# Splitting the last two groups' second-layer products into high and low parts

## The chip, the cores and the metric

The kernel runs on one core of a Trainium2 chip. The metric is the device time of one execution in microseconds (us). Before the change the median of three runs is 255.69 us (255.53 to 255.90).

## What is computed

A vision tower with one block: patches of 32 images are projected to 192 channels and a class token is put in front (37 rows an image); a bidirectional recurrence (RWKV's wkv) and a squared-ReLU layer follow as "attention"; then a mixture of 16 experts, 4 chosen for each row, with a shared expert. The change concerns the second matrix of each expert, which turns 96 hidden values back into 192 channels:

```python
c = (jax.nn.one_hot(idx, E, dtype=w.dtype) * w[..., None]).sum(1)      # routing weights
h = jax.nn.silu(jnp.einsum('th,ehi->tei', x, gWg) + gbg) * (jnp.einsum('th,ehi->tei', x, gWu) + gbu)
out_e = jnp.einsum('tei,eih->teh', h, gWd) + gbd                       # second layer
moe_out = jnp.einsum('te,teh->th', c, out_e)
hs = jax.nn.silu(x @ sWg + sbg) * (x @ sWu + sbu)
shared = hs @ sWd + sbd                                                # second layer, shared
return (moe_out + shared).reshape(orig_shape)
```

All of it is float32.

## The kernel before, in words

The rows are worked on in four groups of 6, 10, 10 and 6 images: groups 0 and 3 have 222 rows in 2 row tiles of 112, groups 1 and 2 have 370 rows in 3 row tiles of 124. Each group passes through stages, and each engine interleaves the stages of several groups:

- **F** (front): patches, first norm, the projections k, v, r (PE), the recurrence with its scans (DVE) and exponentials (ACT), and the output projection.
- **M** (mid): second norm, the squared-ReLU layer (`up`, `mix`), third norm, router logits and the choice of experts (many short DVE operations, the last is `routed`).
- **G** (PE): the first layer of the experts in 14 units of 128 hidden values, unit 0 and 1 the shared expert's (`sgu`), 2 to 13 the experts' (`egu`). `g n` is unit n's gate product, `v n` its value product. Each is five passes over a stack of high and low parts (`from_stack`): operands of type float32r, one pass each in the trace; a float32 product shows as two.
- **Y** (ACT): `e n`, SiLU of the gate. **S** (DVE): `s n`, value times gate into `hid`, which has two slots, n % 2. **X** (DVE): `x n`, times the routing weights that a DMA has spread over the partitions (`gates`); `end` adds the result to the residual `h1`.
- **D** (PE): `d n`, the second layer of unit n, the sum over the units in the PSUM banks `PA`. Its operands are plain float32, 192 weight columns stream against each row tile of `hid`. `cT` transposes the routing weights, which then go to DRAM and come back as `gates`.

The order on each engine is written out by hand in the lists `PE_ORDER`, `ACT_ORDER` and `DVE_ORDER`: "S3:s5" is step s5 of group 3. Each engine works its list off strictly, semaphores are waited for where a step needs data. Unit `v n+1` on PE can only start when `s n` has emptied its PSUM bank, `g n+1` when `e n` has.

`H` steps are products of constants into an unused bank, between PE's first steps (`pe_heat`).

Of the kernel before, what the change touches and what calls it, by code (L numbers as in the profile page):

```python
# [5 lines left out]
F32, F32R = mybir.dt.float32, mybir.dt.float32r  # L6
# [73 lines left out]
BY_PE = 2  # L80


def build(nc, A):
    ctx = ExitStack()
    with ctx:
# [80 lines left out]
        K, V, R = (sb(n, [128, WK]) for n in ("K", "V", "R"))  # L166
        mx = sb("mx", [128, 2 * (WK + 2) + 2 * WK])
        E1 = sb("E1", [128, 2 * (WK + T)])
        S = sb("S", [128, 4 * WS + 2])
        top = sb("top", [128, WK])  # L170
# [35 lines left out]
        c_pad = sb("c_pad", [TP, TILES, CPAD])  # L206

# [76 lines left out]
        out_ready = counted("out_ready", 1)  # L284
        out_stored = [sem(f"out_stored{g}") for g in range(len(GROUP))]
# [300 lines left out]

        def act_gates(act_e, g):
# [216 lines left out]
        def dve_mid(v, g):  # L804
# [13 lines left out]
            if g >= 2:  # L818
                v.wait_ge(out_stored[g - 2], 16 * GROUP[g - 2].tiles)
# [110 lines left out]
        def dve_weighed(v, g):  # L930
# [7 lines left out]

            v.wait_ge(pe_down, at(pe_down, g, UNITS))
            for bank, a, b in G.banks:  # L940
                h = h1[g % 2][0:G.tp, a:b, :]
                last = V_.tensor_tensor(h, h, rows(PA, G, bank, a, b), ALU.add)
            last.then_inc(out_ready, 1)
            yield "end"

        @block.vector
        def _(v):
# [19 lines left out]
            advance(tracks_of(v, dve_low_parts, F=dve_front, M=dve_mid, S=dve_gated, X=dve_weighed), DVE_ORDER)  # L967
# [78 lines left out]
        def pe_heat(pe):  # L1046
# [25 lines left out]
            yield "rstd"  # L1072
            pe.wait_ge(front_step[0], 5)
# [168 lines left out]
        def pe_downs(pe, g):  # L1242
# [6 lines left out]
            if g:  # L1249
                pe.wait_ge(out_ready, at(out_ready, g, 0))  # L1250
            else:
                split(pe, len(PIECES))
            for n in DOWNS:
                if n < SCH:
# [12 lines left out]
                down(G, PA, src, w, n == DOWNS[0], n == DOWNS[-1]).then_inc(pe_down, 1)  # L1267
# [11 lines left out]
def _order(*parts):  # L1279
# [146 lines left out]
```

## Time and profile before

| | |
|---|---|
| median of 3 runs | 255.69 us |
| the profiled execution | 255.63 us |
| its span in the trace | 253.5 us |
| PE busy | 242.6 us, 96% |
| DVE busy | 191.4 us, 76% |
| ACT busy | 151.0 us, 60% |
| POOL busy | 17.9 us, 7% |
| chain that ended last | PE 73%, ACT 9%, DVE 8%, issue 4% |

The table is read so: PE has work nearly all the time, and it makes up most of the chain of waits. Busy time of PE is modelled from the start of each pass, so that short waits between passes don't show in it; starts of neighbouring passes show them. DVE's share is an average over a first half in which it is nearly full and a second half in which it is not. 2.1 us of the execution's time lie outside the span.

### The profile page before, as it was taken

What the parts mean: (1) busy time and instruction counts of PE and PEld (TensorE: products, weight loads), DVE (VectorE), ACT (ScalarE), POOL (GpSimd) and SP (SyncE); (2) the same over time, 40 slices, a digit from 0 to 9 for tenths busy, and PEclk for the clock granted to TensorE, in tenths of its full rate; (3) what the DMA queues carried; (4) which work ended last, traced back from release to release, by engine and by line L of the source; (5) the groups of instructions that cost most, each with busy time, mean ns of one, the idle gap of its engine ahead of it and who ended that gap; (6) DMA issues with size and microseconds to landing.
All of it is one profiled execution on the core that took longest, in us unless ns stands there. A gap on an engine that the chain in (4) does not pass through costs nothing.

```text
span 253.5 us, 4370 instructions
## 1 busy us (share of the span) xinstructions
PE 242.6 (96%) x1508; PEld 222.6 (88%) x1508; DVE 191.4 (76%) x490; ACT 151.0 (60%) x311; POOL 17.9 (7%) x29
## 2 busy tenths in 40 slices
PE   8789899899999999999999999999999999999994
PEld 7677477677588899999999999999999999999993
DVE  5489988999989999999797799877323275843442
ACT  2797899978769999735767862335631341232220
POOL 6100302003101000101100001010000010000000
PEclk9997999999999999999999999999999999999999
DMA  6958271100000430000005510000354000014510
GB/s 170 332 176 309 85 243 62 38 0 0 0 3 10 106 94 13 0 3 0 1 11 157 185 43 1 1 3 0 82 173 136 18 3 0 1 40 92 102 33 27
DMA packets 13165, 17.46 MB, mean 69 GB/s; under 512 B 2359, under 2 KB 11224, under 8 KB 13016
## 3 DMA queue, kind: packets, MB, share of 16 engines
q1 hardware_dynamic: 12872, 17.08, 22.7%
q8 instruction: 12, 0.20, 0.3%
q10 hardware_dynamic: 272, 0.11, 0.2%
q14 instruction: 9, 0.07, 0.1%
HBM read 16.20 MB, written 0.99 MB: 68 GB/s over the span
## 4 chain that ended last, share of the span: by engine, by line
PE 73%; ACT 9%; DVE 8%; issue 4%; DMA 3%; SPq 2%; POOL 0%; DVEq 0%; POOLq 0%
PE PA L998 16%; PE PG L978 16%; PE PG L980 11%; PE PF L998 7%; PE PQ L978 4%; PE PQ L980 3%; PE PX L1029 2%; DMA gates<-c_rows 2%; PE PQ L1049 2%; PE PF L988 1%; PE PG L1149 1%; PE PG L1148 1%; DMA gates<-in_w_k 1%; ACT norm L422 1%; PE PF L1013 1%
## 5 line engine op out<-in xcount | busy, mean ns | idle before, releaser
L584 ACT ACTIVATE act<-PG,columns 128x222 f32<-128x222 f32 (+3 forms) x56 | 28.4, 507 | 58.8 <-PE PG L980 55.1
L978 PE MATMUL PG<-stack,hi_egu 128*128 128x222 f32 (+1 forms) x288 | 62.2, 324 | 0.0
L927 DVE SCALAR_TENSOR_TENSOR hid<-PG,columns,act 128x222 f32<-128x222 f32 (+1 forms) x52 | 27.3, 524 | 28.3 <-PE PG L980 24.8
L998 PE MATMUL PA<-w_ed,hid 128*124 128x192 f32 (+1 forms) x240 | 46.3, 328 | 0.4 <-DVE hid L936 0.3
L978 PEld LDWEIGHTS PG<-stack,hi_egu 128*128 128x128 f32 x288 | 45.6, 190 | 0.7 <-DVE hid L927 0.2
L980 PE MATMUL PG<-stack,lo_egu 128*128 128x222 f32 (+1 forms) x192 | 42.7, 304 | 0.0
L998 PEld LDWEIGHTS PA<-w_ed,hid 128*124 128x124 f32 (+1 forms) x240 | 38.5, 183 | 1.2 <-DVE hid L936 1.2
L980 PEld LDWEIGHTS PG<-stack,lo_egu 128*128 128x128 f32 x192 | 31.8, 190 | 0.0
L396 POOL TENSOR_TENSOR rstd<-var,minus_half 112x2 f32<-112x2 f32 (+3 forms) x12 | 13.9, 1156 | 186.8 <-DVE var L671 186.8
L936 DVE TENSOR_TENSOR hid<-hid,gates 128x222 f32<-128x222 f32 (+1 forms) x48 | 21.9, 462 | 1.8 <-DMA gates<-c_rows 0.9
L998 PE MATMUL PF<-w_down,mix_hid 128*124 128x192 f32 (+1 forms) x120 | 22.8, 326 | 0.0
L998 PEld LDWEIGHTS PF<-w_down,mix_hid 128*124 128x124 f32 (+1 forms) x120 | 19.5, 182 | 0.3 <-issue 0.2
L754 DVE TENSOR_TENSOR_SCAN S<-E,S 128x333 f32<-128x333 f32 (+1 forms) x16 | 16.2, 1064 | 0.3 <-ACT E L501 0.2
L978 PE MATMUL PQ<-stack,hi_up 128*128 128x222 f32 (+1 forms) x72 | 15.3, 321 | 0.0
L1049 PE MATMUL PQ<-still 128*128 128x256 f32 x36 | 11.8, 488 | 2.5 <-ACT h L450 1.4
L552 ACT ACTIVATE relu<-PQ 128x222 f32<-128x222 f32 (+1 forms) x24 | 9.9, 415 | 5.4 <-PE PQ L980 5.3
L1042 PE MATMUL PA<-gates,columns 128*128 128x512 f32 x24 | 12.4, 598 | 0.7 <-ACT lo_egu L414 0.7
L1049 PEld LDWEIGHTS PQ<-still 128*128 128x128 f32 x36 | 8.8, 256 | 4.5 <-ACT h L450 1.8
L778 DVE RECIPROCAL K<-K 128x222 f32<-128x222 f32 (+3 forms) x8 | 12.2, 1531 | 0.1
L978 PEld LDWEIGHTS PQ<-stack,hi_up 128*128 128x128 f32 x72 | 11.3, 191 | 0.3
L422 ACT ACTIVATE norm<-h,shift,rstd 124x192 f32<-124x192 f32 (+1 forms) x20 | 9.6, 538 | 3.1 <-DVE shift L678 3.0
L558 ACT ACTIVATE mix_hid<-relu 128x222 f32<-128x222 f32 (+1 forms) x24 | 10.8, 451 | 0.8
(248 smaller groups left out, 443.1 us busy)
## 6 DMA issues: line engine op xcount, KB each, us to landing
gates<-in_w_egu SPq DMA_DIRECT2D x6, 512.0 KB, 4.8
gates<-c_rows SPq DMA_DIRECT2D x16, 138.8 KB, 2.9
gates<-c_rows SPq DMA_DIRECT2D x16, 92.5 KB, 2.8
gates<-c_rows SPq DMA_DIRECT2D x16, 83.2 KB, 2.4
w_ed<-in_w_ed SPq DMA_DIRECT2D x1, 1152.0 KB, 8.0
gates<-c_rows SPq DMA_DIRECT2D x16, 55.5 KB, 2.6
gates<-in_w_up SPq DMA_DIRECT2D x2, 384.0 KB, 4.0
pat<-in_patches SPq DMA_DIRECT2D x2, 370.0 KB, 4.1
```

The lines of the kernel that those rows point to most:

```text
L396: nc.gpsimd.tensor_tensor(small[n]["rstd"][0:G.tp, 0:cols, 0:G.tiles], small[n]["var"][0:G.tp, 0:cols, 0:G.tiles], minus_half[0:G.tp, 0:co ...
L422: last = nc.scalar.activation(norm[n][0:G.tp, t, :], x[0:G.tp, t, :], ACT.Identity, bias=small[n]["shift"][0:G.tp, col, t:t + 1], scale=sm ...
L584: nc.scalar.activation(act[128 - gate:128, n % 2, 0:G.n], PG[0:gate, gate_bank(n), 0:G.n], ACT.Silu, bias=bias).then_inc(act_silu, 1)
L754: step(V_.tensor_tensor_scan(run(x, d), run(E1[:, d * WK:d * WK + wk], d), run(x, d), 0.0, ALU.mult, ALU.add))
L778: step(V_.reciprocal(K[:, s], K[:, s]))
L927: V_.scalar_tensor_tensor(out, PG[part, 1, 0:G.n], bias, act[part, i, 0:G.n], ALU.add, ALU.mult).then_inc(mul_done, 1)
L936: V_.tensor_tensor(out, out, gates[:, n - SCH, 0:G.n], ALU.mult).then_inc(hid_ready, 1)
L978: mm(out, w_hi[:, slot, cols], x[:, p, 0:G.n], start=(p == 0), stop=False, skip_group_check=True)
L980: last = mm(out, w_lo[:, p, cols], x[:, p, 0:G.n], start=False, stop=(p == 1), skip_group_check=True)
L998: last = mm(tile_out(P, G, t), src[:, G.ts[t]:G.ts[t] + G.tp], w, start=start and t != 1, stop=stop, skip_group_check=True)
L1042: mm(PA[:, s, 0:cols], ident32, raw[n % RING][:, s * cols:(s + 1) * cols], start=True, stop=False)
L1049: mm(PQ[:, 0:256], still[:, 0:128], still[:, :], start=True, stop=True, skip_group_check=True)
```

## The change

1. For groups 2 and 3 (`SPLIT`), the second layer of units 1 to 13 (group 2) and 1 to 12 (group 3) is computed from float32r parts. ACT copies `hid` to `hid_hi` (rounded), DVE subtracts it from `hid` into `hid_lo`. The weights are split once in the same way into `w_both`, whose 384 columns are the high part and the low part side by side. A row tile then takes two passes: `hid_hi` against all 384 columns, `hid_lo` against the 192 columns of the high part. High-times-high and low-times-high add up in the first 192 columns, high-times-low in the next 192. Unit 0 of both groups and unit 13 of group 3 stay in float32.
2. The two halves are added to the residual apart: a new step `low` and the old `end`. Unit 13 of group 3, which writes the bank that `low` reads, waits for `low`. The third row tile of group 2 now has the bank `PX` to itself.
3. `hid` slots come free when `hid_lo` has been made, no longer when the product is done.
4. The buffers of the recurrence share their memory with `w_both`, `hid_hi` and `hid_lo`, so the weights are split after the last group's recurrence.
5. `gated` of groups 2 and 3 no longer waits for the stores of two groups before; `h1` behind it does.
6. Five more `H` steps stand among PE's first steps, and one of them no longer waits.
7. The three lists are written anew from the first mid stage on.

```diff
+SPLIT = (2, 3)
+SPLIT_UNITS = {2: [1, *range(2, UNITS)], 3: [1, *range(2, UNITS - 1)]}
+BLOCKS = ((1, 2), (2, 6), (6, 10), (10, 14))
...
+        w_both = sb("w_both", [128, UNITS - 1, 2 * C], F32R)
+        hid_hi, hid_lo = (sb(n, [128, 2, N], F32R) for n in ("hid_hi", "hid_lo"))
...
+        def wide_out(G, t, cols):
+            return (PA[0:G.tp, t, cols] if t < 2 else PX[0:G.tp, cols])
...
+        def act_split(act_e, g):
+            if g == SPLIT[0]:
+                act_e.wait_ge(z_ready, at(z_ready, LAST, 1))
+                for i, (a, b) in enumerate(BLOCKS):
+                    nc.scalar.activation(w_both[:, a - 1:b - 1, 0:C], whole_downs(a, b), ACT.Copy).then_inc(w_high, 1)
+                    yield f"w{i}"
+            for n in SPLIT_UNITS[g]:
...
+                nc.scalar.activation(hid_hi[:, n % 2, 0:G.n], hid[:, n % 2, 0:G.n], ACT.Copy).then_inc(hid_high, 1)
+                yield f"h{n}"
...
+        def dve_split(v, g):
+            if g == SPLIT[0]:
+                for i, (a, b) in enumerate(BLOCKS):
+                    v.wait_ge(w_high, i + 1)
+                    V_.tensor_tensor(w_both[:, a - 1:b - 1, C:2 * C], whole_downs(a, b), w_both[:, a - 1:b - 1, 0:C].bitcast(F32), ALU.subtract).then_inc(w_both_in, 1)
+                    yield f"w{i}"
+            for n in SPLIT_UNITS[g]:
+                v.wait_ge(hid_high, split_count(g, n))
...
+                V_.tensor_tensor(hid_lo[:, n % 2, 0:G.n], hid[:, n % 2, 0:G.n], hid_hi[:, n % 2, 0:G.n].bitcast(F32), ALU.subtract).then_inc(hid_low, 1)
+                yield f"l{n}"
+            v.wait_ge(pe_down, down_count(g, SPLIT_UNITS[g][-1]))
+            for h, bank in wide_sums(G, g):
+                last = V_.tensor_tensor(h, h, bank[:, :, C:2 * C], ALU.add)
+            last.then_inc(low_added, 1)
+            yield "low"
...
             for n in DOWNS:
+                if g in SPLIT and n in SPLIT_UNITS[g]:
+                    pe.wait_ge(hid_low, split_count(g, n))
+                    for t in range(G.tiles):
+                        here = slice(G.ts[t], G.ts[t] + G.tp)
+                        mm(wide_out(G, t, slice(0, 2 * C)), hid_hi[:, n % 2, here], w_both[:, n - 1, :], start=n == DOWNS[0], stop=False, skip_group_check=True)
+                        last = mm(wide_out(G, t, slice(0, C)), hid_lo[:, n % 2, here], w_both[:, n - 1, 0:C], start=False, stop=n == DOWNS[-1], skip_group_check=True)
+                    last.then_inc(pe_down, 1)
+                    yield f"d{n}"
+                    continue
...
+                if g in SPLIT:
+                    if n and n not in SPLIT_UNITS[g]:
+                        pe.wait_ge(low_added, g - SPLIT[0] + 1)
...
-    "G3:g9 D3:d7 G3:v9 G3:g10 D3:d8 G3:v10 G3:g11 D3:d9 G3:v11 G3:g12 D3:d10 G3:v12 G3:g13 D3:d11 G3:v13 D3:d12 D3:d13",
+    "G3:g8 D3:d5 G3:v8 G3:g9 D3:d6 G3:v9 G3:g10 D3:d7 G3:v10 G3:g11 D3:d8 G3:v11 G3:g12 D3:d9 G3:v12 D3:d10 G3:g13 G3:v13",
+    "D3:d11 D3:d12 D3:d13",
```

What the lists do to the instructions at two places. First PE's last instructions, before: the two G rows in front are `v13` of group 3, the last row `d12` and `d13` together (two row tiles each).

```order
L998 MATMUL PA<-w_ed,hid 112x192 x2
L978 MATMUL PG<-stack_1,hi_egu 128x222 x3
L980 MATMUL PG<-stack_1,lo_egu 128x222 x2
L998 MATMUL PA<-w_ed,hid 112x192 x4
L85 UNCONDITIONAL_BRANCH
```

And now, from `v13` on:

```order
L1063 MATMUL PG<-stack_1,hi_egu 128x222 x3
L1065 MATMUL PG<-stack_1,lo_egu 128x222 x2
L1349 MATMUL PA<-w_both,hid_hi 112x384
L1350 MATMUL PA<-w_both,hid_lo 112x192
L1349 MATMUL PA<-w_both,hid_hi 112x384
L1350 MATMUL PA<-w_both,hid_lo 112x192
L1349 MATMUL PA<-w_both,hid_hi 112x384
L1350 MATMUL PA<-w_both,hid_lo 112x192
L1349 MATMUL PA<-w_both,hid_hi 112x384
L1350 MATMUL PA<-w_both,hid_lo 112x192
L1371 MATMUL PA<-w_ed,hid 112x192 x2
```

`d11` has moved from before `v13` to behind it, so that two split units stand between `v13` and the float32 unit `d13`.

DVE's last instructions, before (`s12`, `x12`, `s13`, `x13`, `end`):

```order
L927 SCALAR_TENSOR_TENSOR hid<-PG,columns,act 128x222
L936 TENSOR_TENSOR hid<-hid,gates 128x222
L927 SCALAR_TENSOR_TENSOR hid<-PG,columns,act 128x222
L936 TENSOR_TENSOR hid<-hid,gates 128x222
L942 TENSOR_TENSOR h_1<-h_1,PA 112x384
```

And now (`s11`, `x11`, `s12`, `x12`, `l11` and `l12`, `s13`, `x13`, `low`, `end`):

```order
L981 SCALAR_TENSOR_TENSOR hid<-PG,columns,act 128x222
L990 TENSOR_TENSOR hid<-hid,gates 128x222
L981 SCALAR_TENSOR_TENSOR hid<-PG,columns,act 128x222
L990 TENSOR_TENSOR hid<-hid,gates 128x222
L1023 TENSOR_TENSOR hid_lo<-hid,hid_hi 128x222 x2
L981 SCALAR_TENSOR_TENSOR hid<-PG,columns,act 128x222
L990 TENSOR_TENSOR hid<-hid,gates 128x222
L1027 TENSOR_TENSOR h_1<-h_1,PA 112x384
L1004 TENSOR_TENSOR h_1<-h_1,PA 112x384
```

The subtractions of two units stand together behind both of their `x` steps, and `low` comes between `x13` and `end`.

The last place is DVE between groups 1 and 2, before (`s13`, `x13`, `end` of group 1, then `s0` to `s3` and `x2` of group 2):

```order
L927 SCALAR_TENSOR_TENSOR hid<-PG,columns,act 128x370
L936 TENSOR_TENSOR hid<-hid,gates 128x370
L942 TENSOR_TENSOR h_1<-h_1,PA 124x384
L942 TENSOR_TENSOR h_1<-h_1,PA 124x192
L927 SCALAR_TENSOR_TENSOR hid_s<-PG,columns,act 64x370
L927 SCALAR_TENSOR_TENSOR hid<-PG,columns,act 128x370 x2
L936 TENSOR_TENSOR hid<-hid,gates 128x370
```

And now:

```order
L981 SCALAR_TENSOR_TENSOR hid<-PG,columns,act 128x370
L990 TENSOR_TENSOR hid<-hid,gates 128x370
L981 SCALAR_TENSOR_TENSOR hid_s<-PG,columns,act 64x370
L997 TENSOR_TENSOR h_1<-h_1,PA 124x384
L997 TENSOR_TENSOR h_1<-h_1,PA 124x192
L981 SCALAR_TENSOR_TENSOR hid<-PG,columns,act 128x370
L1015 TENSOR_TENSOR w_both<-w_ed,w_both 128x4x192 x2
L1023 TENSOR_TENSOR hid_lo<-hid,hid_hi 128x370
L981 SCALAR_TENSOR_TENSOR hid<-PG,columns,act 128x370
```

Two of the four weight subtractions and `l1` now stand between `s1` and `s2` of group 2; the other two stand further ahead, in the choice of experts of group 2.

## Rows read from the trace of the kernel before

**Rows 1.** Stretch: length, busy us of PE, PEld, DVE, ACT, POOL, clock, DMA
```profile
50.00:75.00 25.00, 23.97 (x134) 18.03 (x134) 23.60 (x54) 19.53 (x40) 3.01 (x2) 1.00 0.01 1
75.00:100.00 25.00, 24.28 (x166) 23.09 (x165) 24.22 (x55) 23.80 (x46) 0.85 (x1) 1.00 0.25 57
...
150.00:175.00 25.00, 25.00 (x158) 24.89 (x157) 21.71 (x76) 10.33 (x21) 1.54 (x2) 1.00 0.00 1
...
200.00:225.00 25.00, 25.00 (x158) 24.65 (x156) 16.07 (x56) 6.67 (x15) 0.93 (x1) 1.00 0.01 2
225.00:253.50 28.50, 24.71 (x188) 23.56 (x186) 12.27 (x29) 5.79 (x13) 0.00 (x0) 1.00 0.30 65
```

**Rows 2.** The same view at the start of the kernel, same columns
```profile
20.00:22.00 2.00, 2.00 (x7) 1.55 (x6) 1.97 (x10) 1.68 (x4) 0.00 (x0) 0.52 0.54 217
```

**Rows 3.** Chain of waits, float32 second-layer units: start us, us, engine and line
```profile
203.37 0.97 PE PA L998 x6
...
233.03 0.65 PE PA L998 x4
```

**Rows 4.** Groups by form, PE's weight loads: count, then busy us and mean ns
```profile
L998 PEld LDWEIGHTS PA<-w_ed,hid 128*124 128x124 f32 x144 | 23.7, 187 | 0.2 <-DVE hid L936 0.2
```

**Rows 5.** Timeline of PE, float32r passes, group 2: start us, us
```profile
132.31 0.47 PE L988 MATMUL PF<-hi_rf,stack 128*124 128x192 f32 x3
...
132.84 0.49 PE L988 MATMUL PF<-hi_rf,stack 128*124 128x192 f32 x3
...
134.80 0.68 PE L978 MATMUL PG<-stack,hi_egu 128*128 128x370 f32 x3
...
135.66 0.68 PE L978 MATMUL PG<-stack,hi_egu 128*128 128x370 f32 x3
```

**Rows 6.** The same view, float32r passes with 112 weight columns, group 3
```profile
177.66 0.46 PE L988 MATMUL PF<-hi_rf,stack 128*112 128x192 f32 x3
...
178.15 0.51 PE L978 MATMUL PQ<-stack,hi_up 128*128 128x222 f32 x3
```

**Rows 7.** Groups by form, DVE and ACT: count, busy us, mean ns
```profile
L936 DVE TENSOR_TENSOR hid<-hid,gates 128x370 f32<-128x370 f32 x24 | 12.9, 541 | 0.5
...
L619 DVE TENSOR_TENSOR lo_up<-gates,hi_up 128x768 fp32r<-128x768 f32 x2 | 1.8, 954 | 0.2 <-ACT hi_up L405 0.2
```

**Rows 8.** The same view of ACT
```profile
L558 ACT ACTIVATE mix_hid<-relu 128x370 f32<-128x370 f32 x12 | 6.2, 513 | 0.4
...
L584 ACT ACT_TABLE_LOAD x4 | 5.1, 1283 | 0.1
...
L558 ACT ACTIVATE mix_hid<-relu 128x222 f32<-128x222 f32 x12 | 4.7, 390 | 0.4
```

**Rows 9.** Timeline of one period in group 3 (v, s, next v)
```profile
238.66 0.62 PE L978 MATMUL PG<-stack,hi_egu 128*128 128x222 f32 x3
...
239.54 0.45 DVE L927 SCALAR_TENSOR_TENSOR hid<-PG,columns,act 128x222 f32<-128x222 f32 x1 [0.89 <-PE PG L980]
...
240.42 0.62 PE L978 MATMUL PG<-stack,hi_egu 128*128 128x222 f32 x3
```

**Rows 10.** Timeline where group 3's units begin (g1's last passes, v1)
```profile
225.35 0.38 PE L980 MATMUL PG<-stack,lo_sgu 128*128 128x222 f32 x2
...
225.81 0.59 PE L978 MATMUL PG<-stack,hi_sgu 128*128 128x222 f32 x3
```

**Rows 11.** Timeline of the end (d12, s13, x13, d13, end)
```profile
248.14 0.81 PE L998 MATMUL PA<-w_ed,hid 128*112 128x192 f32 x4
248.34 0.45 DVE L927 SCALAR_TENSOR_TENSOR hid<-PG,columns,act 128x222 f32<-128x222 f32 x1 [0.88 <-PE PG L980]
248.83 0.39 DVE L936 TENSOR_TENSOR hid<-hid,gates 128x222 f32<-128x222 f32 x1
249.27 0.90 PE L998 MATMUL PA<-w_ed,hid 128*112 128x192 f32 x4 [0.32 <-DVE hid L936]
250.21 0.55 DVE L942 TENSOR_TENSOR h<-h,PA 112x384 f32<-112x384 f32 x1 [1.00 <-PE PA L998]
```

More of the change, by code:

```diff
@@ L164, in build @@
             ("rstd", [TP, 2, TILES]), ("shift", [TP, 2, TILES]))) for i in "123")]
[L166 to L170, printed above, removed]
         Zm = sb("Zm", [128, N])
@@ L206, in build, with early @@
         c_pad = sb("c_pad", [TP, TILES, CPAD])
+        with ExitStack() as recurrence_space:
+            def early(name, shape):
+                return recurrence_space.enter_context(nc.sbuf_tensor(name, shape, F32))
+            K, V, R = (early(n, [128, WK]) for n in ("K", "V", "R"))
+            mx = early("mx", [128, 2 * (WK + 2) + 2 * WK])
+            E1 = early("E1", [128, 2 * (WK + T)])
+            S = early("S", [128, 4 * WS + 2])
+            top = early("top", [128, WK])
+        w_both = sb("w_both", [128, UNITS - 1, 2 * C], F32R)
+        hid_hi, hid_lo = (sb(n, [128, 2, N], F32R) for n in ("hid_hi", "hid_lo"))
         PF = pb("PF", [128, 2, 512])
@@ L292, in tile_out, with whole_downs, wide_sums, split_count @@
             return P[0:G.tp, t // 2, (t % 2) * C:(t % 2 + 1) * C]
+        def whole_downs(a, b):
+            return whole["sd"][:, a:b, :] if a < SCH else whole["ed"][:, a - SCH:b - SCH, :]
+        def wide_out(G, t, cols):
+            return (PA[0:G.tp, t, cols] if t < 2 else PX[0:G.tp, cols])
+        def wide_sums(G, g):
+            pairs = (h1[g % 2][0:G.tp, 0:2, :], PA[0:G.tp, 0:2, :]), (h1[g % 2][0:G.tp, 2:3, :], PX[0:G.tp, None, :])
+            return pairs[:G.tiles - 1]
+        def split_count(g, n):
+            return sum(len(SPLIT_UNITS[k]) for k in SPLIT if k < g) + SPLIT_UNITS[g].index(n) + 1
+        def down_count(g, n):
+            return at(pe_down, g, DOWNS.index(n) + 1)
         def advance(tracks, order):
@@ L824, in dve_mid @@
             settle()
+            if g >= 2:
+                v.wait_ge(out_stored[g - 2], 16 * GROUP[g - 2].tiles)
             step(V_.scalar_tensor_tensor(h[rs], gate_r[rs], 0.5, base[g % 2][rs], ALU.mult, ALU.add))
@@ L922, in dve_gated @@
                     since(v, hid_ready, g)
+                elif g in SPLIT:
+                    v.wait_ge(hid_low, split_count(g, n - 2))
                 else:
@@ L1054, in pe_heat @@
                 yield f"early{n}"
-            pe.wait_ge(tok_out, 1)
-            spin()
-            yield "tok"
+            for n in range(4):
+                spin()
+                yield f"tok{n}"
             pe.wait_ge(front_step[0], 1)
@@ L1072, in pe_heat @@
             yield "rstd"
+            for after in ("kt", "rt"):
+                spin()
+                yield after
             pe.wait_ge(front_step[0], 5)
@@ L1266, in pe_downs @@
                     src, w = hid[:, n % 2, :], whole["ed"][:, n - SCH, :]
-                down(G, PA, src, w, n == DOWNS[0], n == DOWNS[-1]).then_inc(pe_down, 1)
+                if g in SPLIT:
+                    if n and n not in SPLIT_UNITS[g]:
+                        pe.wait_ge(low_added, g - SPLIT[0] + 1)
+                    for t in range(G.tiles):
+                        last = mm(wide_out(G, t, slice(0, C)), src[:, G.ts[t]:G.ts[t] + G.tp], w, start=False, stop=n == DOWNS[-1], skip_group_check=True)
+                    last.then_inc(pe_down, 1)
+                else:
+                    down(G, PA, src, w, n == DOWNS[0], n == DOWNS[-1]).then_inc(pe_down, 1)
                 yield f"d{n}"
```

43 lines of the change are left out of this document (36 added, 7 removed), and 114 rows, old and new, of tables (ACT_ORDER, DVE_ORDER, PE_ORDER).

## The prediction

> **What bounds the kernel now.** I read the busy time by stretch first. From 150 us to 225 us PE is busy without a gap, with DVE at 21.7 of 25 us and later at 16.1 [rows 1]; before that, from 50 to 100 us, PE has 1.7 us free (1.03 and 0.72) while DVE is filled to 23.6 and 24.2 of 25. So the kernel has two halves: until about 100 us DVE's list sets the pace, from there to the end PE's. A microsecond of PE work taken from the second half is a microsecond of the result, as long as the engines that feed PE stay ahead. All of the changed products lie in that half (group 2's begin after 180 us, group 3's end at 250). The chain of waits says the same: float32 second-layer units stand on it with their full length, 0.97 us for three row tiles and 0.65 for two [rows 3], which is 323 ns a tile.
>
> **What a tile costs after.** No row shows a 384-column float32r pass beside a 192-column one, so I bound it and take the nearest rows. Narrow pass: five passes of 192 columns with 124 weight columns start 0.53 us apart as a block (132.31 to 132.84), 107 ns each [rows 5]; with 112 weight columns 0.49 (177.66 to 178.15), 98 ns [rows 6]. Their time follows the weight columns, since 192 streaming columns alone would take 80 ns (a float32 tile streams them four times in 323). Wide pass: five passes of 370 columns take 0.86 us (134.80 to 135.66), 171 ns each [rows 5]; scaled to 384 that is 177 ns. A tile then takes 177 + 107 = 284 ns in group 2 and 177 + 98 = 275 in group 3, against 323.
> Group 2 has 13 split units of 3 tiles, 39 x 39 ns = 1.52 us. Group 3 has 12 units of 2 tiles, 24 x 48 ns = 1.15 us. Together -2.67 us.
> Bounds: if only the streaming counted, 161 + 80 = 241 ns, the term would be 63 x 82 = -5.2 us; if one more load of 107 ns showed in each tile (391 ns), 63 x 68 = +4.3. I take the rows of the same type, which have their loads in them, and expect an error of at most 20 ns a tile, 1.3 us.
>
> The float32 records here last 187 ns in weight load [rows 4] and yet a tile takes 323 for four streams of 80: the loads are hidden under the passes in front. The Trainium skill, "TensorE: Matmul & The Clock Gate", Part 3 (The mechanism), says weights load beside running products only when the row group differs. All of these use all 128 rows; by that rule a new tile would take 241 plus two loads of 107, 455 ns, and the change cost 8 us. The trace contradicts it for this kernel, so it gets no chance of its own. The same page, Back-to-back issue gap, gives a warm pass N/2.4 + 2.5 ns: the pair would take 163 + 83 = 245 ns, and the time come to about 250.8. The rows put 171 ns where it has 157 (370 columns) and 107 where it has 83. It stays as a small rival.
>
> **What feeds it.** For each split unit ACT makes a copy and DVE a subtraction. DVE: 0.54 us at 370 columns [rows 7], 0.39 at 222 [rows 11], 13 and 12 times, 11.7 us; the weights are 13 x 192 columns, three blocks of 768 at 0.95 [rows 7] and one small one, about 3.2; `low` twice (0.55 in group 3 [rows 11], some 0.9 in group 2). In all 16 us more DVE. ACT: at most 0.51 and 0.39 a copy [rows 8], 11.4 us with 2.5 for the weights, and two more table loads of 1.28 [rows 8] where the new list takes the exponentials of the last recurrence apart. All of it lies beside PE's work if there is room. In group 2's units DVE then has about 0.6 (`s`, estimated from its 0.45 at 222 columns) + 0.54 + 0.54 = 1.7 us to do for each PE period of 2.6 (ten passes of 171 ns and three tiles of 284), plus the choice of experts; from 200 to 225 us it has 9 us free [rows 1] and gets 5 more. In group 3 it has 0.45 + 0.39 + 0.39 = 1.2 for a period of 1.67 (below). ACT is busy for 5.8 of the last 28.5 us [rows 1] and gets 5. There is room, so cost zero, if the chains between them are not too long; their cost is next.
>
> **Chains in group 3.** Before, one period is 1.76 us (238.66 to 240.42) [rows 9]: two float32 tiles (0.65) and ten passes, so 111 ns a pass and 0.56 for `g` or `v`. After, two tiles take 0.55, the period is 1.67. `s` starts 0.88 us after `v`'s first pass (238.66, 239.54), 0.20 after the place where the next unit's passes begin (0.68 with the late first pass), and takes 0.45 [rows 9]. The new DVE list does most units in pairs: s5 s6 x5 x6 l5 l6, then s7. From the end of s6 that is two x (0.78), the copy of the second on ACT (0.39), its subtraction (0.39) and three hand-overs of 0.04 (end of s13 to x13 [rows 11]): s7 starts 1.68 us later. Unhindered it would start 1.67 - 0.45 = 1.22 later, and v8 comes 0.56 + 0.55 - 0.20 = 0.91 after that, at 2.13; s7 needs 0.45 and a hand-over of it, so 1.63 is in time. It is 0.05 late, less if the two x overlap. For four or five pairs I put 0.1 us.
> Start of group 3: v1 now waits for s0 for 0.24 us (two passes of 112 ns, yet 0.46 us from start to start [rows 10]). In the new list d12 and d13 stand between g0 and g1, so this wait goes; but v3 follows g3 directly now, and 0.20 + 0.45 + 0.05 for s2 is 0.14 more than the 0.56 of g3. Net -0.10.
>
> **The end.** Before, d12 starts at 248.14 and would be over at 248.79; d13 starts at 249.27, held by s13 and x13 [rows 11]: 0.48 us idle. After, v13, d11, d12 and d13 follow, and d13 also waits for `low`, which waits for d12. From v13's slot end d11 and d12 take 1.10, their result is there 0.2 later, `low` takes 0.55: d13 starts at 1.87, and PE has been idle for 0.77. That is +0.29. `end` behind it is the same instruction as before. The dearest case is that the late subtractions hold up s13 by another 0.5.
>
> **Lists and other edits.** The list of DVE holds the same work up to the last units of group 0, so the pace of the first half stays; what PE could gain in it is at most its 1.7 us free [rows 1], what it could lose is open. I put 0, with +1.5 on one side and -1.5 on the other. The `H` steps: at 20 to 22 us PE runs at the lower clock level (0.52, 1.2 GHz), but DVE is busy for 1.97 of these 2 us [rows 2], so filling PE there may change the clock and not the time: 0, at best -0.3. The store wait moves one DVE instruction later; that can only gain, and no row names a store as what DVE waited for: 0.
>
> **Sum.** -2.67 + 0.10 - 0.10 + 0.29 = -2.4 us, rounded. The profiled execution took 255.63 us (253.5 span and 2.1 around it), 0.06 from the median of 255.69, so the forecast is 253.2 us.
>
> **Rivals.**
> - *The first half gives back its waits* (12%): the new lists bring PE's work into the 1.7 us free before 100 us [rows 1]; 253.2 - 1.5 = 251.7. For it speaks that some group-0 units stand earlier in DVE's list; against it that DVE itself has under 1 us in 25 free there.
> - *Streaming alone counts* (4%): 250.8, as above; against it the 370- and 192-column rows [rows 5].
> - *The pair chain becomes the bound* (14%): each hand-over a little longer, 0.3 to 0.4 us late for each of four or five pairs, 1.4 us: 254.6. For it speaks that it fits by almost nothing, against it that hand-overs take 0.04 us in the rows [rows 11].
> - *A tile costs what it cost* (7%): the wide pass cannot hide the narrow one's load; 284 becomes 323, and the end's +0.29 is left: 255.9.
> - *Slower: DVE holds up group 2* (8%): w_both, l1 and the low parts come on top of a DVE that is at 21.7 of 25 us from 150 to 175 [rows 1], with the last recurrence's scan moved ahead. Before s2 of group 2 stand 3.2 + 0.54 = 3.7 us more work. The 3.3 us free there can take nearly all of it if they are free to move; if they are waits inside the choice of experts, PE waits 3.7: 253.2 + 3.7 = 256.9. It decides from 2.4 us of such waiting.
> - The forecast's case (55%): 252.3 to 254.2.
>
> **Chances.** A change of under 0.2% (0.5 us) can't be told from none here. Faster: 55 + 12 + 4 + 14 = 85%, of which I move 1 to no change. Same: 8%. Slower: 8%. The range that leaves out the ends beyond reach is 251.4 to 255.4: it leaves out the streaming case and most of the last two, 19%.
>
> **What would show it.** Right: the two passes of a split tile start 177 and 98 to 107 ns apart from their neighbours; group 3's period is 1.67 us instead of 1.76; PE stays at 25 of 25 us from 125 us on; about 0.8 us idle before d13, ended by DVE's `low`; s7, s9 are not what `v` waits for. Wrong: a narrow pass of over 140 ns; gaps before `v` in group 3 at every second unit; PE free for over 0.3 us in any 25 us between 125 and 225; a first half whose milestones (g0 of group 0, first rows of group 1's mid stage) lie over 0.5 us earlier or later than now.

## The result and the profile after

| | before | after |
|---|---|---|
| median of 5 runs, one chip | 255.62 us (255.47 to 255.90) | 253.35 us (252.99 to 253.91) |
| the profiled execution | 255.63 us | 253.68 us |
| its span | 253.5 us | 251.9 us |
| PE busy | 242.6 us | 240.6 us |
| DVE busy | 191.4 us | 202.8 us |
| ACT busy | 151.0 us | 165.0 us |

The ratio is 0.9914 (95% interval 0.9903 to 0.9925): 0.9% faster. Two later sets on other occasions gave 0.9925 (0.9912 to 0.9937) and 0.9920 (0.9899 to 0.9941). The forecast was 253.2 us.

Not all of the 2.3 us lies in the span of the trace. The median span of the five runs is 251.6 us, 1.9 us less than the 253.5 of the kernel before; in the two later sets it is 252.0 and 251.7, again against 253.5. Some 0.3 us more is execution time outside the span: about 2.1 us in every set of the kernel before, and 1.8 in every kernel made from the changed one, the kernel below without any split among them (255.26 us with a median span of 253.5, where the kernel before has 255.56 and 253.4). So the forecast's -2.4 us, all of it worked out for the span, meets 1.5 to 1.9 us there. What makes the 0.3 us is not known.

The windows of the changed kernel, with the columns of [rows 1]:

```profile
50.00:75.00 25.00, 24.13 (x132) 18.06 (x132) 23.41 (x57) 18.99 (x40) 3.01 (x2) 1.00 0.00 1
75.00:100.00 25.00, 24.41 (x175) 23.69 (x174) 24.39 (x57) 24.34 (x48) 0.85 (x1) 1.00 0.25 57
...
150.00:175.00 25.00, 25.00 (x159) 24.91 (x158) 22.20 (x79) 11.33 (x24) 1.78 (x2) 1.00 0.01 2
...
200.00:225.00 25.00, 24.94 (x167) 24.70 (x166) 19.08 (x66) 11.85 (x25) 0.92 (x1) 1.00 0.02 6
```

PE stays full from 125 to 200 us (the two stretches left out are full as well) and has 0.06 us free in the next stretch. DVE and ACT took their additional work beside it. The first half has 1.46 us free on PE instead of the 1.75 of [rows 1].

What a split tile costs is read from the timeline of PE (start us, then us of the record, line and tile names, number of passes). First one unit of group 2 (its three tiles and the first pass of what follows), then one of group 3:

```profile
221.51 0.35 PE L1349 MATMUL PA<-w_both,hid_hi 128*124 128x384 f32 x1
221.70 0.25 PE L1350 MATMUL PA<-w_both,hid_lo 128*124 128x192 f32 x1
221.79 0.36 PE L1349 MATMUL PA<-w_both,hid_hi 128*124 128x384 f32 x1
...
222.07 0.36 PE L1349 MATMUL PX<-w_both,hid_hi 128*124 128x384 f32 x1
222.27 0.25 PE L1350 MATMUL PX<-w_both,hid_lo 128*124 128x192 f32 x1
222.36 0.43 PE L1349 MATMUL PA<-w_both,hid_hi 128*124 128x384 f32 x1
...
232.82 0.34 PE L1349 MATMUL PA<-w_both,hid_hi 128*112 128x384 f32 x1
232.99 0.25 PE L1350 MATMUL PA<-w_both,hid_lo 128*112 128x192 f32 x1
233.08 0.35 PE L1349 MATMUL PA<-w_both,hid_hi 128*112 128x384 f32 x1
233.27 0.25 PE L1350 MATMUL PA<-w_both,hid_lo 128*112 128x192 f32 x1
233.36 0.51 PE L1063 MATMUL PG<-stack,hi_egu 128*128 128x222 f32 x3
...
234.48 0.34 PE L1349 MATMUL PA<-w_both,hid_hi 128*112 128x384 f32 x1
```

Three tiles start 0.85 us apart as a block: 283 ns each in this unit, about 286 in others. Two tiles of group 3 take 0.54 us, 270 ns each. Within a tile the wide pass takes about 190 ns in group 2 and 180 in group 3, the narrow one 90 in both. The period of group 3 is 1.66 us (232.82 to 234.48; 1.67 over seven periods) where [rows 9] has 1.76. On the chain of waits group 2's last units follow each other in 2.56 us (passes of line 1063 at 213.26, 215.82 and 218.38), in the kernel before in 2.68 (second-layer units at 214.23, 216.91 and 219.59). That is 1.6 us for 13 units and 1.1 for 12, together the 2.7 us of the prediction.

The start of group 3's units, on the engines that feed it. A number in brackets is the idle time just before the row and what ended it:

```profile
229.73 0.69 DVE L990 TENSOR_TENSOR hid<-hid,gates 128x222 f32<-128x222 f32 x2 [1.40 <-DMA gates<-c_rows]
230.16 0.69 ACT L636 ACTIVATE hid_hi<-hid 128x222 fp32r<-128x222 f32 x2 [1.52 <-DVE hid L990]
230.58 0.39 DVE L1023 TENSOR_TENSOR hid_lo<-hid,hid_hi 128x222 fp32r<-128x222 f32 x1 [0.16 <-ACT hid_hi L636]
231.03 0.43 PE L1349 MATMUL PA<-w_both,hid_hi 128*112 128x384 f32 x1 [0.57 <-DVE hid_lo L1023]
```

These four rows are a chain: x2 waits for the transfer that spreads the routing weights, the high part for x2, the low part for the high part, and d2 on PE for the low part. Between x2 and d2 there are now 1.30 us instead of 0.45. The same place in the kernel before, x2 and the weight load of d2 (PEld):

```profile
231.13 0.69 DVE L936 TENSOR_TENSOR hid<-hid,gates 128x222 f32<-128x222 f32 x2 [0.91 <-DMA gates<-c_rows]
231.58 0.60 PEld L998 LDWEIGHTS PA<-w_ed,hid 128*112 128x112 f32 x4 [0.26 <-DVE hid L936]
```

So d2 waited for this transfer before the change too, 0.26 us; in the changed kernel's first profile its weight load waits 0.75. The chain of waits says where the transfer comes from (start us, us):

```profile
223.30 2.43 SPq L374
225.78 0.60 SPq L374
226.42 0.58 SPq L374
227.04 2.60 DMA gates<-c_rows
```

x2 waits for six transfers of this kind. The last one here is issued at 227.04 and lands 2.6 us later; the ones before it follow by about 0.6 us, but the one at 223.30 holds the queue for 2.43. The changed kernel begins to issue 2.0 us earlier than the one before (222.48 instead of 224.48), and yet the last issue comes at the same time as there (227.06). What held the one issue no run shows. My prediction has no term for any of this.

Two more waits at the start of group 3: s0 on DVE, then the weight loads of v1 and v3 (PEld):

```profile
223.56 0.45 DVE L981 SCALAR_TENSOR_TENSOR hid_s<-PG,columns,act 64x222 f32<-64x222 f32 x1 [1.26 <-PE PX L1350]
224.06 0.41 PEld L1063 LDWEIGHTS PG<-stack,hi_sgu 128*128 128x128 f32 x3 [0.24 <-DVE hid_s L981]
226.78 0.41 PEld L1063 LDWEIGHTS PG<-stack,hi_egu 128*128 128x128 f32 x3 [0.17 <-DVE hid L981]
```

v1 waits for s0, and s0 waits for the last product of group 2, d13, which stands just ahead of g1 on PE. v3 waits for s2.

The end (v13's slot ends at 245.61), answering to [rows 11]:

```profile
245.61 0.34 PE L1349 MATMUL PA<-w_both,hid_hi 128*112 128x384 f32 x1
...
246.61 0.25 PE L1350 MATMUL PA<-w_both,hid_lo 128*112 128x192 f32 x1
246.90 0.55 DVE L1027 TENSOR_TENSOR h<-h,PA 112x384 f32<-112x384 f32 x1 [0.17 <-PE PA L1350]
247.60 0.88 PE L1371 MATMUL PA<-w_ed,hid 128*112 128x192 f32 x4 [0.74 <-DVE h L1027]
248.58 0.55 DVE L1004 TENSOR_TENSOR h<-h,PA 112x384 f32<-112x384 f32 x1 [1.13 <-PE PA L1371]
```

L1027 is `low`, L1004 `end`. d13 starts 1.99 us after v13's slot; a narrow pass takes 0.09, so PE is idle from 246.70 to 247.60, 0.90 us, against 0.48 before.

### The profile page after: what moved, and what is told of

It is laid out like the page before. It is cut to its first block, busy times and chain, and to the rows that moved or that the text cites. A ratio compares the mean times of both kernels' runs of the same rounds, so it can differ in the third digit from the quotient of the medians.

```text
span 251.9 us, 4509 instructions
## 1 busy us (share of the span) xinstructions
PE 240.6 (96%) x1518; PEld 220.1 (87%) x1518; DVE 202.8 (81%) x522; ACT 165.0 (65%) x342; POOL 19.0 (8%) x29
## 4 chain that ended last, share of the span: by engine, by line
PE 71%; ACT 7%; DVE 2%; SPq 2%; DMA 2%; issue 1%; DVEq 0%; ACTq 0%
PE PG L1063 17%; PE PG L1065 11%; PE PA L1083 9%; PE PF L1083 8%; PE PQ L1063 4%; PE PA L1349 3%; PE PQ L1065 3%; PE PX L1114 2%; SPq L374 2%; PE PA L1350 1%; PE PG L1237 1%; PE PF L1098 1%; PE PX L1063 1%; PE PF L1073 1%; PE PG L1236 1%
## 5 line engine op out<-in xcount | busy, mean ns | idle before, releaser
L1063 PE MATMUL PG<-stack,hi_egu 128*128 128x222 f32 (+1 forms) x288 | 60.4, 318 | 0.0
L981 DVE SCALAR_TENSOR_TENSOR hid<-PG,columns,act 128x222 f32<-128x222 f32 (+1 forms) x52 | 27.2, 522 | 12.6 <-PE PG L1065 10.5
L427 POOL TENSOR_TENSOR rstd<-var,minus_half 112x2 f32<-112x2 f32 (+3 forms) x12 | 15.0, 1253 | 183.2 <-DVE var L723 183.2
L1083 PE MATMUL PA<-w_ed,hid 128*124 128x192 f32 (+1 forms) x120 | 23.4, 327 | 0.0
L1083 PEld LDWEIGHTS PA<-w_ed,hid 128*124 128x124 f32 (+1 forms) x120 | 19.3, 183 | 0.0
L636 ACT ACTIVATE hid_hi<-hid 128x370 fp32r<-128x370 f32 (+1 forms) x25 | 10.9, 449 | 10.1 <-DVE hid L990 6.0
L1023 DVE TENSOR_TENSOR hid_lo<-hid,hid_hi 128x370 fp32r<-128x370 f32 (+1 forms) x25 | 11.5, 468 | 7.3 <-ACT hid_hi L636 7.2
L1349 PE MATMUL PA<-w_both,hid_hi 128*124 128x384 f32 (+1 forms) x50 | 15.8, 355 | 0.6 <-DVE hid_lo L1023 0.6
L1134 PE MATMUL PQ<-still 128*128 128x256 f32 x46 | 12.4, 420 | 1.1 <-POOL still L421 1.1
L1350 PE MATMUL PA<-w_both,hid_lo 128*124 128x192 f32 (+1 forms) x50 | 12.6, 251 | 0.0
```

Source lines behind the costliest of these rows:

```text
L427: nc.gpsimd.tensor_tensor(small[n]["rstd"][0:G.tp, 0:cols, 0:G.tiles], small[n]["var"][0:G.tp, 0:cols, 0:G.tiles], minus_half[0:G.tp, 0:co ...
L981: V_.scalar_tensor_tensor(out, PG[part, 1, 0:G.n], bias, act[part, i, 0:G.n], ALU.add, ALU.mult).then_inc(mul_done, 1)
L1063: mm(out, w_hi[:, slot, cols], x[:, p, 0:G.n], start=(p == 0), stop=False, skip_group_check=True)
L1083: last = mm(tile_out(P, G, t), src[:, G.ts[t]:G.ts[t] + G.tp], w, start=start and t != 1, stop=stop, skip_group_check=True)
L1134: mm(PQ[:, 0:256], still[:, 0:128], still[:, :], start=True, stop=True, skip_group_check=True)
L1349: mm(wide_out(G, t, slice(0, 2 * C)), hid_hi[:, n % 2, here], w_both[:, n - 1, :], start=n == DOWNS[0], stop=False, skip_group_check=True)
```

## The experiments

Theory: the gain is the float32r tiles, less what the start and the end of group 3 give back; the lists and the `H` steps bring nothing. Rivals: the lists bring the gain; the narrow pass costs the same wherever it stands. The ratios are to the kernel before on the same chip. For scale: the changed kernel has 0.9914, 0.9925 and 0.9920. It was not run in one set with the lists alone, the first kernel with the old first half, the three narrow passes and the kernel without the `H` steps, so these four are compared with it by these ratios.

### The lists alone

New lists and `H` steps up to the end of group 1, old lists behind, no group split:

```diff
-SPLIT = (2, 3)
+SPLIT = (9,)
...
```

> The new lists (and the new steps on TensorE in the first 25 us) up to the end of group 1, then the old lists for groups 2 and 3, and no group in high and low parts: the second-layer products of all groups stay as they were before. My theory: the lists alone are worth nothing, because the first 225 us end at the same time in both traces but for 0.2 us; it expects 255.4 to 255.7 us, within 0.2% of the kernel before. Rival (the lists brought the gain, or part of it): 254.6 us or less. Second rival (the lists cost time, and the high and low parts are worth more than the 2.3 us that the two kernels differ by): 256.2 us or more.

Measured: 255.26 us, ratio 0.9986 (0.9977 to 0.9995). That is 0.36 us, at the edge of what can be told: a sixth of the gain, by the interval up to a quarter. It lies outside the span, whose median is 253.5 us here and 253.4 in the kernel before. In the profiles v1 of group 3 starts at 225.74 here and at 225.81 in [rows 10]. The lists did not bring the gain.

### The parts behind the old first half, twice

Old lists and no added `H` steps up to group 1's end, new ones from there. The casts of the weights have to stand somewhere in the old part of ScalarE's list:

```diff
-Y1:e8 M2:ln3 M2:tr3 M2:logits Y1:e9
+Y1:e8 T2:w0 M2:ln3 M2:tr3 M2:logits T2:w1 T2:w2 Y1:e9
```

> The reverse: the old lists (and the old steps on TensorE in the first 25 us) up to the end of group 1, then the new lists for groups 2 and 3 with the products in high and low parts; the three steps that cast the weights' parts ahead of group 2 are put into the old lists. My theory: all of the change's gain is here, so 253.2 to 253.6 us, as the changed kernel. If the lists bring part of the gain, it lies above 254 us; if they cost, below 253.0 us.

Measured: 256.95 us, ratio 1.0054 (1.0042 to 1.0067). My theory missed. By the expectation's wording this is the case above 254 us, in which the lists bring part of the gain; but it is slower than the kernel before, which a share of the gain can't explain. The windows of PE and the timeline of ScalarE and PE in this kernel show where:

```profile
160.00:182.00 22.00, 18.98 (x122) 17.96 (x121) 14.97 (x59) 10.45 (x21) 0.69 (x1) 1.00 0.00 1
```

```profile
160.16 0.36 ACT L625 ACTIVATE w_both<-w_sd 128x192 fp32r<-128x192 f32 x1 [1.85 <-DVE Zt L838]
160.43 1.41 ACT L453 ACTIVATE norm<-h,shift,rstd 124x192 f32<-124x192 f32 x3
161.90 0.85 PE L1098 MATMUL PF<-columns,norm 124*128 124x124 f32 x6 [1.52 <-ACT norm L453]
...
166.84 1.56 ACT L625 ACTIVATE w_both<-w_ed 128x768 fp32r<-128x768 f32 x2
168.42 0.57 ACT L615 ACTIVATE act<-PG,columns 128x370 f32<-128x370 f32 x1
```

`w_both` shares its memory with the recurrence's buffers, so the first cast waits 1.85 us for the last product that reads them, and the norm of the mid stage is queued behind it (160.43, in the old kernel at 158.31). The other two casts hold up a SiLU by 1.56 us. PE waits 1.52 us for that norm and, by the view of its waits, 1.2 for that SiLU; it loses 3.0 us of 22. I had taken ScalarE's low share (10.3 of 25 us in [rows 1]) for room; in a strict queue there is room only at the places where the queue waits anyway. So I put the casts there, and VectorE's two behind the end of group 1's units:

```diff
-Y1:e8 T2:w0 M2:ln3 M2:tr3 M2:logits T2:w1 T2:w2 Y1:e9 Y1:e10 Y1:e11
+Y1:e8 M2:ln3 M2:tr3 M2:logits Y1:e9 T2:w0 Y1:e10 T2:w1 T2:w2 Y1:e11
```

> As e7_split (the old lists up to the end of group 1, then the new ones with high and low parts), but the steps that cast the weights' parts stand elsewhere in the old lists: ScalarE's three behind the SiLU of units 9 and 10 of group 1, where its rows in the trace before show 1.2 and 2.1 us of idle time, instead of ahead of the norm and of unit 9's SiLU; VectorE's two behind the end of group 1's units, where it has 3 us of idle time. In e7_split ScalarE's first cast waited 1.85 us for the Zt product of frame 3 (VectorE L838) with the norm queued behind it, and the next two (1.56 us) stood ahead of unit 9's SiLU; TensorE then waited 3.0 us between 150 and 182 us. If that placing is all that e7_split lost: 253.3 to 253.9 us, no wait of TensorE between 150 and 182 us, and the new lists of the first half are worth nothing but the room for these casts. Rival (the old first half leaves VectorE or ScalarE too late for group 2 with its parts, wherever the casts stand): 255 us or more, with the wait of TensorE in group 2.

Measured: 253.26 us, ratio 0.9904 (0.9889 to 0.9920), as fast as the changed kernel. The same stretch and the same places:

```profile
160.00:182.00 22.00, 22.00 (x148) 21.86 (x147) 16.78 (x63) 10.73 (x22) 0.70 (x1) 1.00 0.03 9
```

```profile
166.03 0.35 ACT L625 ACTIVATE w_both<-w_sd 128x192 fp32r<-128x192 f32 x1
167.35 0.57 ACT L615 ACTIVATE act<-PG,columns 128x370 f32<-128x370 f32 x1 [0.96 <-PE PG L1065]
167.81 1.57 ACT L625 ACTIVATE w_both<-w_ed 128x768 fp32r<-128x768 f32 x2
170.03 0.57 ACT L615 ACTIVATE act<-PG,columns 128x370 f32<-128x370 f32 x1 [0.64 <-PE PG L1065]
```

The rows behind the casts still have idle time before them, so nothing was displaced, and PE is full. Together: the new first half is worth nothing by itself, five steps at other places in two lists were worth 3.7 us. VectorE's two moved in the same run; that ScalarE's three were the ones that cost is read from PE's two waits above, not from a run of its own.

### Three narrow passes a tile

```diff
-mm(wide_out(G, t, slice(0, 2 * C)), hid_hi[:, n % 2, here], w_both[:, n - 1, :], start=n == DOWNS[0], ...)
+mm(wide_out(G, t, slice(0, C)), hid_hi[:, n % 2, here], w_both[:, n - 1, 0:C], start=n == DOWNS[0], ...)
+mm(wide_out(G, t, slice(C, 2 * C)), hid_hi[:, n % 2, here], w_both[:, n - 1, C:2 * C], start=False, ...)
```

> The changed kernel with each 384-column pass split into two passes of 192 columns over the same weights (hid_hi), so that a tile is three narrow passes instead of one wide and one narrow; the arithmetic is the same. It asks what a narrow pass costs when its neighbours are narrow too, which was my reading of the old kernel's 107 ns (124 weight columns) and 98 ns (112). By that reading a tile is 321 ns or 294 ns, where the changed kernel's trace has about 286 and 268: (35 x 39 + 26 x 24) ns = 2.0 us more, 255.3 us. Rival: a narrow pass costs the 88 ns that its records are apart in the changed kernel whatever stands beside it, so 264 ns a tile: 1.0 us less, 252.4 us. Second rival: only columns count, no change, 253.3 us.

Measured: 255.52 us, ratio 0.9994 (0.9985 to 1.0003), nearly all of the gain gone: by the ratios 1.8 to 2.0 us above the changed kernel. The first theory holds; copies, subtractions, slots and lists are the same here, only the wide pass is missing. PE's timeline of this kernel, group 2's last two tiles and a unit of group 3:

```profile
222.31 0.27 PE L1349 MATMUL PA<-w_both,hid_hi 128*124 128x192 f32 x1
222.42 0.27 PE L1350 MATMUL PA<-w_both,hid_hi 128*124 128x192 f32 x1
222.53 0.27 PE L1351 MATMUL PA<-w_both,hid_lo 128*124 128x192 f32 x1
222.63 0.27 PE L1349 MATMUL PX<-w_both,hid_hi 128*124 128x192 f32 x1
...
222.97 0.51 PE L1063 MATMUL PG<-stack,hi_sgu 128*128 128x222 f32 x3
...
234.25 0.26 PE L1349 MATMUL PA<-w_both,hid_hi 128*112 128x192 f32 x1
234.34 0.26 PE L1350 MATMUL PA<-w_both,hid_hi 128*112 128x192 f32 x1
...
234.83 0.51 PE L1063 MATMUL PG<-stack,hi_egu 128*128 128x222 f32 x3
```

Six narrow passes take 0.66 us with 124 weight columns (222.31 to 222.97), 110 ns each, and 0.58 us with 112, 97 ns each: the prices of [rows 5] and [rows 6]. The same 576 columns a tile take 330 and 290 ns in three passes, 286 and 270 in two. The change lives on the wide pass.

### Without the `H` steps

```diff
-            for n in range(4):
-                spin()
-                yield f"tok{n}"
+            pe.wait_ge(tok_out, 1)
+            spin()
+            yield "tok"
...
-            for after in ("kt", "rt"):
-                spin()
-                yield after
```

> The changed kernel without the five added steps of spinning products on TensorE in the first 25 us (they are as in the kernel before). My theory: these steps hold the granted clock at full between 18 and 22 us, where it fell to half before, but nothing waits for TensorE there (VectorE's steps of the first half stand at the same time in both traces), so the time stays at 253.2 to 253.6 us, while the granted clock of TensorE falls to about 0.5 for some us near 20 us. Rival: the clock there is worth time, 253.9 us or more.

Measured: 253.37 us, ratio 0.9914 (0.9901 to 0.9928), the time as expected. The clock was not: the same window as [rows 2], of this kernel, has the full clock (the figure before the last two):

```profile
20.00:22.00 2.00, 1.85 (x9) 1.29 (x7) 1.97 (x10) 1.64 (x5) 0.00 (x0) 1.00 0.57 231
```

So the `H` steps are not shown to be what kept the clock up. The 0.52 of [rows 2] need not be in every execution: the profiled one has a mean granted clock of 0.993, and of the 21 runs of the kernel before in this set two have 0.993 and the others up to 1.000, with 255.37 and 255.91 us for the two and a median of 255.56 for all. Either way DVE is busy for 1.97 of these 2 us, and the time does not follow.

### The end, the start, and both

The spare bank `PX` for the last unit, so that d13 need not wait until `low` has read the other bank. What it still waits for is group 2's `low`, which reads `PX`:

```diff
+                for h, bank in wide_sums(G, g):
+                    V_.tensor_tensor(h, h, bank[:, :, 0:C], ALU.add).then_inc(high_added, 1)
...
-                        pe.wait_ge(low_added, g - SPLIT[0] + 1)
+                        pe.wait_ge(low_added, 1)
...
+                        out = PX[0:G.tp, t * C:(t + 1) * C] if apart else wide_out(G, t, slice(0, C))
```

> The changed kernel, but the last unit's second-layer products of group 3 (d13, bfloat16) go to the spare bank PX, which group 2's odd units used, instead of into PA beside the sums; VectorE adds PA's high part while TensorE works on the last units, and PX at the end. So d13 need not wait until group 3's low parts have been read from PA. In the changed kernel's trace d13 stands at 247.60 us after 0.74 us of waiting on VectorE's h (v13's slot ended at 245.61), and the wait on the low parts' read lies in the same stretch. If the low parts' read is what holds d13: d13 0.5 to 0.8 us earlier, the last addition at the end too, 252.6 to 252.9 us. Rival (the h of the last unit through SiLU, gate and weight holds it whatever the bank): within 0.2 us of the changed kernel, and the wait on L1027 stays in the trace. Second rival (the added addition stands in VectorE's queue ahead of the last h): slower, 253.6 us or more.

Measured: 252.97 us, ratio 0.9894 (0.9880 to 0.9907), just above the 252.6 to 252.9 expected. (d13 is float32, not bfloat16 as the expectation has it.) The timeline of DVE and PE at the end of the kernel with both changes, whose end is built alike:

```profile
246.36 0.91 PE L1387 MATMUL PX<-w_ed,hid 128*112 128x192 f32 x4
246.47 0.55 DVE L1041 TENSOR_TENSOR h<-h,PA 112x384 f32<-112x384 f32 x1 [0.16 <-PE PA L1364]
247.06 0.55 DVE L1009 TENSOR_TENSOR h<-h,PA 112x384 f32<-112x384 f32 x1
247.64 0.55 DVE L1013 TENSOR_TENSOR h<-h,PX 112x384 f32<-112x384 f32 x1
```

d13 follows without a wait, beside the low part's addition. Now three additions on DVE, 0.58 to 0.59 us apart, are the end.

The routing weights of each expert apart:

```diff
...
-                 v.wait_ge(gates_in[(n - SCH) // 3], 16 * len(SPANS) * (g + 1))
+                 if g == LAST and n < SCH + 3:
+                     v.wait_ge(chunk_in[n - SCH], 16 * 2)
+                 else:
+                     v.wait_ge(gates_in[(n - SCH) // 3], 16 * len(SPANS) * (g + 1))
```

> The changed kernel, but VectorE's first step of group 3 that needs routing weights (x2) waits for the two transfers that bring its own expert's row (a semaphore for each of the first three experts) instead of all six of the first period. In the changed kernel's trace x2 waits 1.40 us for these transfers (they are issued 0.60 us apart and x2 stands at 229.73), and d2 on TensorE waits 0.57 us for what follows x2. If that chain holds d2: x2 about 2 us earlier, d2's wait gone, the end 0.4 to 0.6 us earlier, 252.7 to 252.9 us. Rival: d2 is then held by g3's SiLU or by h of the pair behind it, the time stays at 253.3 us with the wait moved to d3 or d4.

Measured: 253.31 us, ratio 0.9905 (0.9890 to 0.9920). The expected 252.7 to 252.9 was missed. The time is the rival's, but its sign, the wait moved to d3 or d4, is not in the profile: PE waits nowhere between v3 and d12.

> Both changes of the two kernels above together: the spare bank for the last unit, and a semaphore for each expert's routing weights in group 3's first period. They lie at the start and at the end of group 3, whose middle is 1.67 us a pair with TensorE never waiting. If both waits are on the path their gains add: 0.5 + 0.5 us, 252.2 to 252.5 us. Rival (an earlier start of group 3 is taken back by VectorE's own rate in the pairs): the time of the better of the two alone.

Measured: 252.75 us, ratio 0.9888 (0.9875 to 0.9902), the lowest median here, yet above the 252.2 to 252.5 expected. It is 0.22 us below the spare bank alone, with intervals that overlap; that the two gains add is not shown.

> The changed kernel once more, on the chip of these experiments, as what they are to be compared with: 253.1 to 253.6 us, 0.9914 of the kernel before as measured first (0.9903 to 0.9925).

Measured: 253.78 us (0.9925), above the expected range by 0.2. Against it the three are 0.81, 0.47 and 1.03 us faster.

> The changed kernel beside it on the same chip: 253.2 to 253.9 us.

Measured: 253.49 us (0.9920).

Differences of half a microsecond are near what these medians can tell, but the profiles tell more. The table gives the start of the kernel's first norm on ScalarE, of v1 of group 3 and of the last addition, and how long d2's weight load waited (all us):

| kernel | first norm | v1 | last addition | v1 to last addition | d2's weight load waits |
|---|---|---|---|---|---|
| before | 10.03 | 225.81 | 250.21 | 24.40 | 0.26 |
| changed, first profile | 10.00 | 224.06 | 248.58 | 24.52 | 0.75 |
| changed, again | 10.49 | 224.65 | 248.90 | 24.25 | 0.49 |
| changed, third | 10.27 | 224.35 | 248.01 | 23.66 | none |
| without `H` steps | 10.15 | 224.26 | 247.92 | 23.66 | none |
| old first half, casts in the way | 10.30 | 228.13 | 251.79 | 23.66 | none |
| old first half, casts placed | 10.64 | 224.65 | 248.31 | 23.66 | none |
| gates apart | 10.30 | 224.65 | 248.31 | 23.66 | none |
| spare bank | 10.62 | 224.69 | 247.85 | 23.16 | none |
| both | 10.23 | 224.50 | 247.64 | 23.14 | none |

The undisturbed stretch is 23.66 us in every kernel that shares it. The spare bank takes 0.50 us off it. d2's wait appears in two profiles of three of the same program and costs 0.59 and 0.86 us where it does, 0.1 more than its length. Here is the row of x2 in the third profile, where the transfer landed earlier:

```profile
229.02 0.69 DVE L990 TENSOR_TENSOR hid<-hid,gates 128x222 f32<-128x222 f32 x2 [0.40 <-DMA gates<-c_rows]
```

With the semaphores apart x2 doesn't wait for the transfer: it starts 4.19 and 4.18 us after v1 in the two profiles that have them apart, the earliest of all. But in the other kernels without a wait of d2 the transfer landed in time as well, so no profile shows the semaphores removing a wait that would have been there, and 0.47 us between four and five runs is thin. v1 itself moves by 0.6 us between the three profiles of the changed kernel. Most of that arises before 10.5 us: the first norm starts at 10.00, 10.27 and 10.49, and from it to v1 they take 214.06, 214.08 and 214.16 us, where the kernel before took 215.78.

## Why the prediction was right, point by point

- **A tile.** Predicted 284 and 275 ns, measured about 286 and 270. By the periods the term is 13 x 0.12 + 12 x 0.09 = 2.7 us, as predicted. (In group 3 the ten passes behind a split pair take 0.02 us longer than before, which eats the 5 ns a tile.) The split inside was off: 177 + 107 and 177 + 98 were forecast, about 190 + 90 and 180 + 90 are there. That the sum came out is in part luck. The narrow pass behind a wide one starts its successor sooner than in a row of narrow ones, and the wide one takes longer; the sum hides it. The three-pass kernel shows that the prices from [rows 5] and [rows 6] are right where the neighbours are narrow. The rule that I had weighed and set aside (the Trainium skill, "TensorE: Matmul & The Clock Gate", Part 3, The mechanism: loads run beside products only in another row group) would have made an estimated 455 ns of a tile; the measured 286 speaks against it. Of the same page's Back-to-back issue gap I had used the warm gap of N/2.4 + 2.5 ns, which would have made an estimated 245; the page calls it the isolated gap and says that in a stream the loads count too, and the measured 286 agrees with that.
- **What feeds it.** DVE's busy time grew by 11.4 us where I had 16. The added rows do sum to 16 (the low parts of `hid` alone 11.5), but records of neighbours overlap and count once, as in x2's row above: two operations of 0.39 in 0.69. ACT's grew by 14.0 (I had 13.9 and two table loads of 1.28; the two are there, ten instead of eight). PE stayed full: the slower rival, DVE holding up group 2, did not come. That the risk was real is shown by the first kernel with the old lists: the same work at other places made 256.95 us, through ScalarE's queue, where that rival had 256.9 through VectorE's.
- **Chains in group 3.** Predicted +0.10 us for the pairs, measured 0: the period is 1.66 to 1.67 us throughout. For the start I had put -0.10, of it -0.24 because v1's wait was to go, as d12 and d13 stand between g0 and g1. This step was wrong: s0 waits for d13 (1.26 us, ended by PE, in the rows above), so that v1 waits 0.24 us as before. The other part, v3 behind g3, was forecast at +0.14 and is 0.24: 0.15 of waiting (227.07 in the third profile, 226.92 would do) and 0.09 because v3's block then takes 0.65 us instead of 0.56. From the first norm to v1 the profiles give -1.72, -1.62 and -1.70 us; I had -1.76, of it -1.52 for the tiles.
- **The missed term.** Behind x2 stand two more operations and two hand-overs, 0.85 us, and x2 is the first step that waits for a DMA. I worked out the chain from `s`, where no DMA is, and read d2 nowhere, though the kernel before shows its wait. It costs 0 to 0.86 us, by how late the transfer lands, and 0.33 of the same kind stood in the kernel before.
- **The end.** +0.29 predicted, +0.42 measured (0.90 us idle instead of 0.48). The wait is the one named, for DVE's `low`; v13's slot to d13 takes 1.99 us and not 1.87: from the end of `low` (247.45) to d13 (247.60) pass 0.15 us, for which I had 0.02.
- **From v1 on, summed.** Without the missed wait -0.74 us (24.40 to 23.66): -1.1 for twelve shorter periods, +0.24 for v3, +0.46 for the end (0.42 and 0.04 more from d13 to the last addition), and -0.33 because the 24.40 of the kernel before hold a wait of d2 themselves (0.24 between the passes and 0.09 behind it). Predicted was -1.15 + 0.10 + 0.14 + 0.29 = -0.62. Three terms are off by 0.1 to 0.2 us and one was not in the sum; they nearly cancel.
- **Lists and `H` steps.** 0 predicted; none in the span for the one (0.36 us in all, 0.3 of it outside the span), none for the other. My reading of why the clock is full in that window was not borne out.
- **The sum.** -2.4 us predicted, -2.3 measured in the first set and about -1.85 and -2.1 in the later ones. In the span it is -1.9, -1.5 and -1.8. The tiles are right to 0.1 us. That the sum comes so near is partly luck. v1's wait that stayed, the longer waits at v3 and at the end, and in two of three profiles the wait of d2 took away more than forecast. The pairs that cost nothing, the wait of d2 that the kernel before had itself, and the 0.3 us outside the span gave back, and none of these three was in the sum.

## What to carry to other kernels

Price a new pass by rows with the same neighbours, and check the sum of the pair rather than each pass: the same columns cost 286 ns in two passes and 330 in three. In an engine with a fixed queue, added work is free only at places where the queue waits already; a low busy share says nothing on that, and 1.9 us of misplaced casts on ScalarE, with VectorE's two, cost 3.7 us here. When steps are added behind an operation that waits for a transfer, put the whole lengthened path from the transfer's landing to the bounding engine into the sum, and look first whether the kernel before already waits there. Compare spans as well as times: part of a difference can lie outside the span.

## What the runs showed that I had not expected

- A 192-column float32r pass with 124 weight columns takes 110 ns among its like and about 90 behind a 384-column one, which itself takes about 190.
- One of the six issues on SP ahead of x2 held the queue for 2.43 us in the first profile and for 1.84 in the second, the others for 0.3 to 0.6; in the third profile the longest took 1.32, and the transfer landed in time for d2.
- Execution time outside the span is 1.8 us in the changed kernel and all made from it, 2.1 in the kernel before.
- The landing of the same routing-weight transfer, and with it x2, differs by 1 us between profiles of one program (229.02, 229.73, 230.06), while the compute stretches agree to 0.01 us (23.66 five times).
- The granted clock was 0.52 from 20 to 22 us in the profile of before, and 1.00 there in the profiles of the three kernels without the added `H` steps as well as in those with them.
